# The normalised x made by GpSimd behind its square roots, in an attention and expert kernel

## What is computed

```python
def _layernorm(x, axis=-1, eps=1e-05):
    m = jnp.mean(x, axis=axis, keepdims=True)
    v = jnp.var(x, axis=axis, keepdims=True)
    return (x - m) / jnp.sqrt(v + eps)
# attention, in chunks of 128 rows; q, k through elu(.) + 1
scores = jnp.where(mask, jnp.einsum('bhcd,bhkd->bhck', q_c, k_c), 0.0)
num = jnp.einsum('bhck,bhke->bhce', scores, v_c) + jnp.einsum('bhcd,bhde->bhce', q_c, S)
# experts: gate_logits = xn @ gate_w.T + gate_b + expert_bias, the argmax picks one
h = jax.nn.relu(jnp.einsum('bsd,df->bsf', x, w1[e]) + b1[e])
y = jnp.einsum('bsf,fd->bsd', h, w2[e]) + b2[e]
# result: x + attention(xn) + experts(xn)
```

## Time and profile before

| what | us |
|---|---|
| median of 3 executions | 512.15 |
| lowest, highest | 511.81, 512.28 |
| span of the profiled execution, first to last instruction | 510.7 |

### The profile page before, as it was taken

How to read it: one execution, slowest core, us unless ns; L and a number is a source line. 1 busy time by engine, 2 the same in 40 slices (tenths; PEclk the granted TensorE clock), 3 DMA queues, 4 the chain that set the end, 5 groups by cost and what they waited for, 6 DMA issues and landing times.

```text
span 510.7 us, 17892 instructions
## 1 busy us (share of the span) xinstructions
PE 489.6 (96%) x6293; PEld 406.0 (79%) x6293; DVE 403.7 (79%) x881; ACT 280.9 (55%) x540; POOL 266.8 (52%) x465
## 2 busy tenths in 40 slices
PE   8699999999999999999998799999999999999996
PEld 8578887888878888788877688888888888888884
DVE  3798999999999999999889277766776776776775
ACT  3448887788877888877885033333332333333331
POOL 4345667767667676676663523344334344344222
PEclk9899999999999999999999799999999999999999
DMA  8525565565555655655442612122212212210000
GB/s 263 196 66 160 175 194 165 180 221 167 183 180 178 206 179 172 195 177 178 143 138 102 194 33 82 48 85 68 68 53 67 85 51 81 73 51 28 23 17 1
DMA packets 34306, 62.91 MB, mean 123 GB/s; under 512 B 5677, under 2 KB 10030, under 8 KB 34096
## 3 DMA queue, kind: packets, MB, share of 16 engines
q1 hardware_dynamic: 29232, 49.17, 30.1%
q0 software_dynamic: 4992, 12.60, 8.2%
HBM read 51.00 MB, written 13.50 MB: 126 GB/s over the span
## 4 chain that ended last, share of the span: by engine, by line
PE 82%; DVE 6%; POOL 5%; issue 4%; ACT 2%; DMA 1%; DVEq 0%; POOLq 0%; ACTq 0%
PE ps L654 21%; PE ps L667 20%; PE ps L401 7%; PE ps L443 6%; PE ps L472 5%; PE ps L516 5%; PE ps L456 4%; PE ps L486 4%; PE ps L419 3%; PE ps L502 2%; PE ps L623 2%; PE ps L426 1%; PE ps L508 1%; DVE AR L706 1%; PE ps L384 1%
## 5 line engine op out<-in xcount | busy, mean ns | idle before, releaser
L654 PEld LDWEIGHTS ps<-AR,W 128*128 x1872 | 132.2, 99 | 40.4 <-issue 1.5
L654 PE MATMUL ps<-AR,W 128*128 128x128 f16 x1872 | 156.9, 221 | 1.0 <-ACT AR L1227 0.9
L667 PE MATMUL ps<-W,ST 128*128 x624 | 150.5, 326 | 0.0
L1236 ACT ACTIVATE ST<-ST 128x512 f16<-128x512 f32 x78 | 49.2, 630 | 118.9 <-DVE ST L1056 118.9
L1056 DVE SCALAR_TENSOR_TENSOR ST<-ps,TAs,B1S 128x512 f32<-128x512 f32 x78 | 58.3, 748 | 52.7 <-PE ps L654 42.8
L1385 POOL DMA_INDIRECT out<-AR x39 | 39.7, 1017 | 109.2 <-DVE AR L1088 101.5
L1323 POOL TENSOR_TENSOR W<-ST,W 128x512 f16<-128x512 f32 x64 | 74.7, 1167 | 27.8 <-ACT W L1170 21.5
L762 DVE TENSOR_TENSOR AR<-ps,CT 128x512 f32<-128x512 f32 x128 | 81.9, 682 | 2.1 <-PE ps L443 2.1
L1068 DVE SCALAR_TENSOR_TENSOR ST<-ST 128x512 f16<-128x512 f32 x78 | 53.6, 687 | 15.6 <-ACT ST L1236 15.6
L1380 POOL DMA_INDIRECT AR<-scr,AR x39 | 48.7, 1250 | 30.6 <-DVE AR L1088 12.1
L401 PE MATMUL ps<-xT,WA 128*128 128x128 f16 x768 | 49.5, 222 | 3.7 <-ACT xT L1120 2.9
(11 more groups left out here) (147 smaller groups left out, 784.1 us busy)
## 6 DMA issues: line engine op xcount, KB each, us to landing
ST<-in_w SPq DMA_DIRECT2D x128, 256.0 KB, 4.1
scr<-XR SPq DMA_DIRECT2D x32, 256.0 KB, 2.1
XR<-in_x SPq DMA_DIRECT2D x32, 128.0 KB, 4.6
AR<-in_b SPq DMA_DIRECT2D x1, 1024.0 KB, 4.9
AR<-in_wall SPq DMA_DIRECT2D x2, 388.0 KB, 3.8
AR<-scr,AR POOLq DMA_INDIRECT x39, 3.7
out<-AR POOLq DMA_INDIRECT x39
ST<-in_cst SPq DMA_DIRECT2D x1, 576.0 KB, 4.4
```

What stands on the lines that cost most here:

```text
L654: a = e.matmul(dst, W[:, off:off + 57472][:, bass.ds(place_of(s), 128)], XT16[s % 2][:, xl * 256 + k * 128:xl * 256 + (k + 1) * 128], star ...
L667: a = e.matmul(PS[4 + s % 2][:, 0:w], src[h % 4][:, fs], W[:, off:off + 57344 + w][:, bass.ds(place_of(s), w)], start=(f == 0 and w == 512 ...
L1236: e.activation(HH[h % 4], H32[h % 2], ACT.Relu).then_inc(a_hh, 1)
```

## The change

`nb` is taken out of VectorE's function and put into GpSimd's, with the same operands. In its place there it stands in each step behind `km(p - 2)` and, in even steps, behind `nn_end`; ahead of the routing counts, `w_lo` and `xl(p)`. `nb(0)` stands behind `nn_end(1)` and ahead of the copy of the identity. A wait for the load of x is added, since GpSimd had not waited for it. The kernel's other engines are as before.

```diff
@@ vector
-            def nb(c):
-                e.wait_ge(S["nn"], c // 2 + 1)
-                if c >= 1:
-                    e.wait_ge(S["xl"], c)
-                e.tensor_scalar(XN, XR[c % R][:, 256:512], mv[:, c % 4, 0:1],
-                                rsn[:, c // 2 % 2, 0, c % 2:c % 2 + 1],
-                                ALU.subtract, ALU.mult).then_inc(S["nb"], 1)
...
-            nb(0)
...
-                if on(p) and p > 0:
-                    nb(p)
                 w_max(2 * p)
@@ gpsimd
+            def nb(c):
+                e.wait_ge(S["nn"], c // 2 + 1)
+                e.wait_ge(d_x[c % R], 16 * (c // R + 1))
+                if c >= 1:
+                    e.wait_ge(S["xl"], c)
+                e.tensor_scalar(XN, XR[c % R][:, 256:512], mv[:, c % 4, 0:1],
+                                rsn[:, c // 2 % 2, 0, c % 2:c % 2 + 1],
+                                ALU.subtract, ALU.mult).then_inc(S["nb"], 1)
...
                     nn_end(1)
+                    nb(0)
...
                     nn_end(p + 1)
+                if on(p) and p > 0:
+                    nb(p)
```

## The result

The changed kernel takes 511.06 us (median of 9 executions, 510.3 to 512.02) against 511.85 for the kernel before on the same chips; the ratio is 0.9977, 95% interval 0.9967 to 0.9986, which is 1.2 us (0.7 to 1.7). On another chip it was 510.10 against 511.74, ratio 0.9966 (0.9956 to 0.9976), 1.7 us (1.2 to 2.3). The forecast was 510.2, in the range 507.4 to 511.9. The profiled execution has a span of 510.2 us, where before had 510.7.

A forecast was written before the change was run, and what follows sets the result against it. The prediction took PE (TensorE) to bound the kernel, with VectorE mattering only where PE waits for it. The start's 1.2 us and the steady part's 0.7 made 1.9 us, from 512.15 to 510.2 us, range 507.4 to 511.9.

The forecast's parts named there:

- What GpSimd gets: Each moved 128x256 nb was to take 0.45 us on GpSimd, ends 0.29 and 0.69.
- The start, 1.2 us: First chunks: earlier phi(0) gives 1.0 us and PE's vanished wait for phi(1) 0.28; bounds 0.4 and 1.7.
- Step (a): Start: nb(0) ends on GpSimd at 9.37, the reduction begins at 8.05, ScalarE's weights at 9.85 instead of 10.77: 0.9 us.
- Step (c): Start, chunk 2: nb(2) ends on GpSimd at 21.35 instead of 22.48, and relu(1) starts at 21.95 instead of 23.04.
- The steady part, 0.7 us: Attention steps: fewer PE waits for the residual sum and phi give 0.7 us; bounds 0 and 1.6.
- The room on GpSimd, 2.1 us: Attention steps: GpSimd idles about 2.1 us a step; each 0.1 us of nb beyond that costs 2.8 us.
- The first: Rival: the start's gain is eaten and the contention only moves; start 0.4, steps 0, time 511.7 us; chance 0.25.
- the second: Rival: PE's half-clock spell from about 286.5 to 293 us may not come, saving 2.8 us: 507.4 us; chance 0.17.
- The third: Rival: GpSimd becomes the bound if the new form exceeds 2.1 us; 514.5 us at 2.2; chance 0.06.

The follow-up runs named there:

- The run with four forms: Changed kernel with four forms of nb on GpSimd from chunk 3 on, from both scalars per partition to one operation with a constant: 28 steps 218.97 us.
- The start alone: Against the kernel before, only nb(0), nb(1) and nb(2) moved to GpSimd, the rest on VectorE: 511.46 us, ratio 0.9995.
- The kernel that was held apart: Against the kernel before, nb stays on VectorE and GpSimd's first w_lo of a step waits until nb is done: 513.81 us, ratio 1.0047.

## Why the prediction was right, and where its terms were wrong

The time lay in the range, and the direction held. The sum of 1.9 us came out as 1.2 and 1.7 us in two comparisons, but its two terms were both mis-sized, in opposite ways: 1.2 forecast and 0.3 measured for the start, 0.7 and 1.8 for the steps. That the errors nearly cancelled is luck. All three things by which the prediction said it would be wrong came: the new form took over 1 us, the third q/k came later than 27 (27.34), and the clock was low at another time. VectorE's busy time fell by 14.1 us, not 19, in part because the operation of line 876 takes 2.3 us more in all.

**What GpSimd gets.** The step that failed most: 0.45 us taken, upper end 0.69, measured 1.23. I drew a line through a cast of 128 columns and an operation of two columns and applied it to another operation. The run with four forms shows that the operation itself is the dear part: 0.85 us for its barest form. The bound from above was no bound either: a two-input subtraction of the same width (0.688) is not dearer than this one-input form. The nearest rows were near by shape, not by kind. The measured 1.23 us is three times VectorE's 0.40. The Trainium skill ("GPSIMD Engine Reference", Engine selection) puts GpSimd at about twice VectorE's time for two inputs and near line rate for one; this operation with one input does not bear the second out, and the measurement decides.

**The start, 1.2 us.** Step (a) held for VectorE (reduction at 7.95), failed for ScalarE, since `nb(0)` ends at 10.33 instead of 9.37: 0.1 us instead of 0.9. Step (c) failed the same way: `nb(2)` ends at 23.15, later than the 22.48 before. The start alone measured 0.3 us (0.2 slower to 0.7 faster); the lower bound of 0.4 lies within that. The reasoning that these chains bound the start was in part right: kernels that shorten them on VectorE begin the first q/k 0.8 us earlier. At the third q/k, with the clock spell at the same place, 0.4 us of that is left (27.55 against 27.97), and why it is not more stays open.

**The steady part, 0.7 us.** It measured 1.8, above the upper bound of 1.6. The mechanism was named rightly, the stall of `nb` behind `w_lo` in steps 10, 18 and 26. The wrong step was that it would come back at the routing operations of the same step, so that only 0.1 of each 0.3 us was counted. It did not, and these steps gave 1.28 us together instead of 0.3; the steps behind them, counted at 0.1 to 0.2 each, gave 0.19 each. The reason hangs on the first error: because `nb` on GpSimd takes 1.23 us, `w_lo` starts that much later and misses them. It came back in steps 12, 20 and 28 instead, at another routing operation, where it cost 0.14 us in all at most. With `nb` at 0.85 us `w_lo` starts 0.20 us after the second operation of step 10; with 0.45 us it would have started 0.2 us ahead of it and might have met it. That was not run. The kernel that was held apart has such meetings and takes 7.72, 8.25 and 8.25 us for these steps instead of 7.53.

**The room on GpSimd, 2.1 us.** The steady cover held for 1.23 us, but the threshold was of the wrong kind. At 2.46 us the cost was 25.8 us over 28 steps instead of 10, with GpSimd busy 88% of the time: ScalarE's queue waits in the middle of its step for `nb`, and half-clock spells that fell behind gaps of PE come on top.

**The rivals.** The first, start 0.4 and steps nothing, is right for the start and wrong for the steps. The clock did as the second said in part: at the entry into the expert part the changed kernel's first trace has half the clock from about 287.4 to 290.8 and no longer from 286.5 to 293; its second trace has it from 284.4 to 291.2. The spells come at other places from execution to execution, and no gain is to be claimed for it. Nor did the short spell save time: from the 32nd q/k to the last instruction the first trace takes 255.1 us, the second 254.4. Over all traces this last part, whose code is the same, takes 253.6 to 255.8 us, and the traces with the short spell at its entry are not the fast ones throughout; what scatters it is open. The third did not come.

## What to carry to other kernels

Look for the instances of an operation that last two or three times its minimum, ask what the other engine ran then, and ask what stands behind it in the queue: seven of 32 operations were stalled, three of them had the bound engine waiting behind them and carried 1.7 of 1.8 us, and reordering two instructions in those steps gave the same gain. Price an operation on GpSimd by a row of the same operation there, never by another kind with like shape, and test a late operation against the queue that waits for it, not against the engine's idle share.

## What the runs showed of the hardware

- A 128x256 fp32 operation with one input and two scalars per partition takes 1.23 us on GpSimd and 0.40 on VectorE. With one scalar per partition 1.15, with two constants 1.07, with one operation and a constant 0.85.
- Some VectorE operations that start while a two-input operation of GpSimd runs last until that one ends: `nb`, 0.41 becomes 1.23; routing operations with both inputs in SBUF, 0.21 becomes 0.81 and 0.29 becomes 1.11. Others are not held: in the trace of the kernel before, the masked copies and the residual sum, which read PSUM, and the statistics and largest values, with one input, take the same time beside such an operation as without it (0.68 us for the masked copies, in 42 cases beside one). It goes the other way too: `nb(1)` on GpSimd took 1.77 us beside VectorE's two-input low halves. Beside GpSimd's one-input `nb` the two-input routing operations took 0.22 to 0.40.
- In thirteen of the fourteen traces a spell of half the clock (1.2 GHz instead of 2.4) began between 17.1 and 20.7 us, in or behind the idle stretch of PE that ends at 18.57 us, after 2.9 us, in the trace of the kernel before. In one it began at 28.0 us; there PE had been busy for 0.35 us from 24 to 26. Where one fell on full PE work, the step took 8.65 us instead of 7.06.
